# A GNN kernel's fused stage: each gather on GpSimd waits until the one two places ahead has landed

## The reference

```python
# layer 0, edges with 64 features
messages = concat([x[senders], edges64]) @ W_message
agg = segment_sum(messages, receivers)
h = layer_norm(relu(agg) + x) ; nodes = mlp_with_skips(h, 3 layers)
x1 = layernorm(x + layer_norm(x + nodes))
# layer 1, edges with 128 features: attention over the neighbours
h = lrelu(x1 @ w_W + w_b) ; edge_h = lrelu(edges128 @ ew_W + ew_b)
e_ij = concat([h[tgt], h[nbr], edge_h]) @ a_W + a_b
alpha = segment_softmax(e_ij, tgt)
out = layernorm(x1 + lrelu(segment_sum(alpha * h[nbr], tgt)))
```

## Time and profile before

| | |
|---|---|
| median of 3 runs | 6498.25 us (6482.75 to 6502.19) |
| span of the profiled execution | 6510.1 us |
| TensorE busy | 4187.0 us, 64% |
| VectorE busy | 3490.4 us, 54% |
| GpSimd busy | 3530.3 us, 54% |
| ScalarE busy | 1870.4 us, 29% |
| granted TensorE clock, mean | 0.820 of full speed |
| gathers of the fused stage (line 750) | 1785, 1789.7 us on GpSimd |

### The profile page before, as it was taken

How to read it: one execution, slowest core, us unless ns; L and a number is a source line. 1 busy time by engine, 2 the same in 40 slices (tenths; PEclk the granted TensorE clock), 3 DMA queues, 4 the chain that set the end, 5 groups by cost and what they waited for, 6 DMA issues and landing times. The chain is left out here.

```text
span 6510.1 us, 83702 instructions
## 1 busy us (share of the span) xinstructions
PE 4187.0 (64%) x17113; PEld 3084.5 (47%) x17114; DVE 3490.4 (54%) x11262; ACT 1870.4 (29%) x5506; POOL 3530.3 (54%) x3618
## 2 busy tenths in 40 slices
PE   3767777776777777777777835555555555555555
PEld 2545555554555545555555524444444444444444
DVE  6555556555555555565556644444444444444444
ACT  2222222222222222222222213333333333333333
POOL 3555555554555545555555426666666666666664
PEclk8888888988898888888888867777777777777777
DMA  3444444443444434444444623333333333533332
GB/s 115 116 115 119 113 117 125 116 115 111 120 116 119 118 110 116 113 122 114 114 116 125 110 62 91 92 91 91 92 90 92 93 92 90 91 90 93 91 91 69
DMA packets 546631, 679.29 MB, mean 104 GB/s; under 512 B 341873, under 2 KB 379359, under 8 KB 546221
## 3 DMA queue, kind: packets, MB, share of 16 engines
q0 software_dynamic: 172416, 464.26, 26.7%
q1 hardware_dynamic: 359216, 201.09, 11.8%
q10 hardware_dynamic: 14976, 13.69, 0.6%
HBM read 648.41 MB, written 29.43 MB: 104 GB/s over the span
## 5 line engine op out<-in xcount | busy, mean ns | idle before, releaser
L750 POOL DMA_INDIRECT rows<-in_x,picked x1785 | 1789.7, 1003 | 1692.3 <-ACT picked L942 1138.5
L1658 POOL DMA_INDIRECT nbr<-nodetab,nbr_idx x1700 | 1609.8, 947 | 1030.1 <-issue 460.5
L781 PE MATMUL bank<-w_edge,feats 128*128 128x258 f32 x3264 | 1122.3, 434 | 631.0 <-ACT bank L923 360.4
L796 PE MATMUL bank<-rows,hot 128*128 128x320 f32 x3570 | 1358.4, 480 | 54.2 <-issue 47.3
L1688 PE MATMUL bank<-nbr,w 128*128 128x258 f32 x3400 | 1044.3, 471 | 289.2 <-issue 152.6
L923 ACT COPY bank<-b_edge 128x258 f32<-128x258 f32 x1635 | 610.4, 378 | 2113.9 <-DVE unused L1151 1597.1
L1151 DVE SCALAR_TENSOR_TENSOR unused<-bank,a_relu 128x258 bf16<-128x258 f32 x1632 | 686.2, 422 | 952.3 <-remote 522.8
L1688 PEld LDWEIGHTS bank<-nbr,w 128*128 128x128 f32 x3400 | 803.3, 244 | 487.6 <-issue 195.5
L781 PEld LDWEIGHTS bank<-w_edge,feats 128*128 128x128 f32 x3264 | 622.9, 213 | 861.1 <-ACT bank L923 416.5
L1720 ACT ACTIVATE w<-off,logit 128x128 f32<-128x128 bf16 x1700 | 523.6, 388 | 1490.5 <-DVE logit L1791 1146.8
L796 PEld LDWEIGHTS bank<-rows,hot 128*128 128x128 f32 x3570 | 759.4, 214 | 277.0 <-issue 126.4
(11 more groups left out here) (347 smaller groups left out, 3943.4 us busy)
## 6 DMA issues: line engine op xcount, KB each, us to landing
feats<-in_edge SPq DMA_DIRECT2D x408, 256.0 KB
rows<-in_edge SPq DMA_DIRECT2D x255, 128.0 KB, 2.6
rows<-in_x,picked POOLq DMA_INDIRECT x1785
nbr<-nodetab,nbr_idx POOLq DMA_INDIRECT x1700
rows<-in_edge SPq DMA_DIRECT2D x153, 160.0 KB
nodetab<-tab ACTq DMA_DIRECT2D x52, 129.0 KB
x_blk<-in_x SPq DMA_DIRECT2D x52, 128.0 KB
x_rows<-u_n ACTq DMA_DIRECT2D x52, 128.0 KB
```

Source lines behind the costliest of these rows:

```text
L750: pool.indirect_dma_start(out=rows[:, STARTS[j] + s, 0:D], out_offset=None, in_=a["x"], in_offset=bass.IndirectOffsetOnAxis(ap=picked[j][: ...
L781: mm(y, feats[:, f0 * P:(f0 + 1) * P], w_edge[:], start=False, stop=True, skip_group_check=True).then_inc(o["y_ready"], 1)
L796: ins = mm(S_PS, hot[j % HR][:, s - STARTS[j], :], rows[:, s, :], start=(s == 0), stop=(s == SA - 1), skip_group_check=True)
L1658: pool.indirect_dma_start(out=nbr[:, TOFF[u] + k, :], out_offset=None, in_=nodetab, in_offset=bass.IndirectOffsetOnAxis(ap=nbr_idx[u][:, k ...
```

## The change

The semaphores of the gathers no longer belong to batches. There are five, used in turn: gather `s` of a pass (0 to 34) adds to `x_in[s % 5]`. 35 is a multiple of five, so each semaphore rises by 112 a pass, and `landed(p, s)` gives the semaphore and the count at which gather `s` of pass `p` has landed. Before each gather but the first two of a pass GpSimd waits for `landed(p, s - 2)`. TensorE waits before a batch for its last two gathers, in place of the batch's one count.

```diff
-            x_in = [sem(f"x_in{j}", ctx) for j in range(NB_SUMS)]
+            x_in = [sem(f"x_in{r}", ctx) for r in range(5)]
...
+            UNDER_WAY, XR = 2, 5
+            assert SA % XR == 0 and UNDER_WAY < XR
...
+            def landed(p, s):
+
+                return x_in[s % XR], p * (SA // XR * 16) + (s // XR + 1) * 16
...
                 def gathers(p, *batches):
                     for j in batches:
                         wait_alone(pool, (o["picked_ready"], p * NB_SUMS + (j + 1)), (o["summed"], p * NB_SUMS + (j + 1)))
-                        for s in range(SUMS[j]):
+                        for s in range(STARTS[j], STARTS[j] + SUMS[j]):
+                            if s >= UNDER_WAY:
+                                wait_alone(pool, landed(p, s - UNDER_WAY))
                             pool.indirect_dma_start(
-                                out=rows[:, STARTS[j] + s, 0:D], out_offset=None, in_=a["x"],
-                                in_offset=bass.IndirectOffsetOnAxis(ap=picked[j][:, s:s + 1].bitcast(U32), axis=0),
-                            ).then_inc(x_in[j], 16)
+                                out=rows[:, s, 0:D], out_offset=None, in_=a["x"],
+                                in_offset=bass.IndirectOffsetOnAxis(ap=picked[j][:, s - STARTS[j]:s - STARTS[j] + 1].bitcast(U32), axis=0),
+                            ).then_inc(x_in[s % XR], 16)
...
                         if s == STARTS[j]:
-                            size = SUMS[j] * 16
-                            pe.wait_ge(x_in[j], p * size + size)
+                            for last in range(s + SUMS[j] - UNDER_WAY, s + SUMS[j]):
+                                pe.wait_ge(*landed(p, last))
                             pe.wait_ge(e_in[j], p * 16 + 16)
```

## The result

The changed kernel takes 6438.12 us (median of 4 runs, 6430.82 to 6451.28) against 6500.22 us (4 runs, 6482.75 to 6507.75): ratio 0.9911, 95% interval 0.9891 to 0.993. The change saves 62 us, 0.9%, where 530 were forecast, over eight times as much. The time lies inside the range given, 5740 to 6800, but only because that range was stretched to a rival's price; the range of the forecast's own mechanism, 5740 to 6210, is missed. Its profiled execution has a span of 6439.0 us, 71.1 less than before.

What follows compares the result with a forecast made beforehand. Slow spells beside GpSimd's gather runs were taken to set the 71.5 us pass. 49 x (71.5 - 61.0) = 515 us, first pass 25, stage's end -10: together 530 off 6510.1, 5980 profiled, say 5970; range 5740 to 6800.

Steps and rivals of the forecast that it cites:

- (a): GpSimd's gathers waiting for the landing two places ahead: 1.56 to 1.81 us each against 1.25, 56.6 to 65.4 a pass.
- the pair: Two gathers on GpSimd take one landing, 2.35 to 2.85 us, plus one start, 0.77: 3.12 to 3.62 us.
- (b): If a fused-stage pass stayed at 71.5 us, the gathers' waits would be hidden in slack and the time unchanged.
- (c): Wait instructions: free on GpSimd; TensorE's eight more a pass cost 0 to 40 us, taken as 0.
- (d): Slow spells of TensorE beside GpSimd's gather runs cost 18.0 us a pass and all but vanish when runs are broken.
- The drain of 1.65 us a gather: Each gather leaves something that drains at a fixed rate, 1.65 us a gather; a cadence about that slow avoids spells.
- First and last pass: Fused stage's ends: 25 us gained in the first pass, 10 us lost where the DMA engines are full at the end.
- The slower one: Rival: spells ignore short pauses and last as long as GpSimd works; 77.2 us a pass, 6780 us; chance 0.33.
- Its other form: No spell, but landing plus start over 4.0 us pushes a pass past 71.5 us; within the slower side's 0.33.
- No change: Rival: spells hang on the gathers' number or the code's place, not spacing; 6480 to 6518 us, chance 0.13.
- Half the gain: Rival: spells get shorter but stay, 65.5 to 71 us a pass; 6210 to 6478, about 6340 us; chance 0.12.
- The rule of the Trainium skill: A DMA never contends with a compute engine, so gathers cannot hold up TensorE and the time would stay; ranked below.

Runs made afterwards that it cites:

- e3_one: The changed kernel with each gather waiting for the one just ahead, on a chip without spells: 8874.14 us, 1.7959 of the kernel before.
- e6_two: The changed kernel itself, two gathers under way, on a chip without spells: 5895.78 us against 4941.78 for the kernel before, ratio 1.1931.
- Four under way: The changed kernel with gathers waiting for the one four ahead, on a chip without spells: 4912.66 us, 0.9941 of the kernel before.
- e15: The kernel before without its fused stage's gathers, on a chip with spells: 5423.05 us against 6512.17, ratio 0.8334.
- Breaks: The changed kernel, only each batch's first gather waiting two ahead, others four: 5231.7 us (1.0587 of before) without spells, 6156.98 (0.9463) with.
- e12: The changed kernel, only each batch's first gather waiting two ahead, others four, on a chip without spells: 5231.7 us, 1.0587 of the kernel before.
- thirds: The changed kernel, every third gather waiting two ahead, others four, on a chip with spells: 5960.34 us, 0.9344 of the kernel before.
- narrow: The changed kernel gathering 64 of 256 columns, on a chip with spells: 6099.85 us, 0.9549 of the kernel before.
- three under way: The changed kernel with gathers waiting for the one three ahead: 5103.6 us (1.0327 of the kernel before) without spells, 6231.77 (0.9796) with.
- e5_before: The kernel before, unchanged, traced on a chip without spells: 4937.47 us in one run.

## Why the prediction was right or wrong

**(a) GpSimd's cost of a gather under the waits: wrong, and the step that failed.** Forecast 1.56 to 1.81 us a gather and a pass of 56.6 to 65.4, measured 1.93 and 70.2. The term is the pair: 3.12 to 3.62 us forecast, 3.86 measured (2 x 1.93). A lone one takes 3.5 to 3.58 (e3_one), inside the forecast. I had added a landing and a start from two single rows of the kernel before and taken the sum to hold for two under way; with two it does not hold, and steps of 3.56 stand beside steps of 4.18. What lengthens them is not shown. The scatters were not sized too small. Among passes 6 to 49 two gathers take 3.94 us where no scatter stands between them and 4.48 where one does, so a scatter adds some 0.5 us and not the 1.0 forecast, and the pass is 35 x 1.97 + 2 x 0.5 = 70. The 9 us a pass above the forecast 61 are the gathers' alone. In the span, 459 us are missing (5980 forecast, 6439 measured), and 49 passes of 69.9 instead of 61 are 438 of them. The upper ends, 65.4 and 6210 us, would still have been 228 us off. (By the terms written out, 56.6 and 65.4 us a pass give 5753 and 6184, not 5740 and 6210; nothing hangs on it.)

**(b) Hidden if a pass stayed at 71.5.** Not tested as such: the pass is GpSimd's. That rests on e6_two, where nothing else can hold it: 69.5 us with a free pass of 50.

**(c) The waits as instructions cost nothing: right.** Four under way has nearly all the waits and takes what the kernel without gathers takes, 4912.66 and 4913.08 us.

**(d) The slow spells: cause and price right, the condition roughly, on this kind of chip.** The gathers cause them (e15). Their price was put at 18.0 us a pass from one last pass; it is 71.1 - 50.2 = 20.9. They go when the stream thins: no "remote" waits in the changed kernel, excess 0.7 us. The drain of 1.65 us a gather was worked out from two runs of rows; that the runs bear it out roughly is more than two rows could promise. Breaks at (1828.2 + 925.8) / 1785 = 1.54 us a gather (e12) still has an excess, thirds at (1814.5 + 1205.0) / 1785 = 1.69 has three tenths of the "remote" waits left, narrow at 1.77 has 11 us of them from 400 to 2600 us, the changed kernel none. Whether anything drains no run shows. What was not seen is that they do not exist on the other kind of chip, where the same change is pure loss.

**First and last pass.** The first came 26.0 us earlier, forecast 25. The end cost 28.2 us where 10 were put: TensorE waits in the last pass for gathers that were issued as late as in any other, and loses its short pass of 53.5 us. The stage's last gather started at 3714.69 us before, 4.8 us after the 50th closing line; now it starts 68.5 us after it, 13.2 us before the end of the last pass:

```profile
3675.60 0.95 POOL L758 DMA_INDIRECT rows<-in_x,picked  x1 [0.53 <-issue]
```

The two together are +2 us, forecast -15.

**The rivals.** The slower one (spells as long as GpSimd works) fell: the spells went. Its other form, no spell but landing plus start over 4.0 us, was missed narrowly, 3.86 us and two scatters making 70.2 of 71.5 us; this is where most of the gain went. "No change" fell by mechanism. "Half the gain" covers the time, 6210 to 6478, but its mechanism, shorter spells, is not what happened here; it is what three under way and breaks do. The rule of the Trainium skill weighed there ("SBUF — State Buffer", "Who interferes with whom"), that a DMA does not contend with a compute engine, fits the chips where the gathers cost 31 us of 4944. Where they cost 1089 of 6512 something that this rule leaves out holds the engines up; that it is a port of the SBUF no run shows.

## What to carry to other kernels

A throttle's cost is the cycle of what it waits for, divided by the number under way, but the cycle changes with that number: it was 3.58 us with one, 3.86 with two, 4.4 with three. Measure it at the number you mean to use; landing and start taken from single rows gave 9 us a pass too little here. When the aim is to thin a stream, waiting at every third item costs less than waiting at every one (61.7 us a pass against 70.2) and took most of the spells away. Spread the waits evenly: with about the same mean pace, but all of the waits for the second one ahead in one half of the pass, 65.6 us were left. And take the profile on more than one chip before tuning against a stall whose cause is not in the program: here the same edit is worth -0.9% and +19.3%.

## What the runs showed of the hardware

Chips of two kinds run one program in 4942 and in 6364 to 6512 us, 29 to 32% longer, and the difference hangs on GpSimd's gathers beside the engines' work: without them the fused stage agrees to 0.2 us. What a spell is, is open. The prediction described it by TensorE's weight loads, but in the kernel before it does not begin there. Timelines of TensorE and VectorE in the slow step of the earlier trace rows:

```profile
1660.03 1.05 PE L855 MATMUL bank<-h_t,w_mlp 128*128 128x128 f32 x8
1660.91 0.60 PE L781 MATMUL bank<-w_edge,feats 128*128 128x258 f32 x2
```

```profile
1660.01 0.68 DVE L1171 TENSOR_TENSOR hot<-iota,rel 128x512 f32<-128x512 f32 x1
1666.10 0.61 DVE L1218 SCALAR_TENSOR_TENSOR h_t<-bank,b_low,s_t 128x128 f32<-128x128 f32 x2 [5.40 <-remote]
1666.62 0.41 DVE L1151 SCALAR_TENSOR_TENSOR unused<-bank,a_relu 128x258 bf16<-128x258 f32 x1
```

VectorE stands still for 5.4 us, though what lines 1218 and 1151 read is ready at about 1661.1 and 1661.5 (the ends of matmuls are modelled). TensorE's loads 0.71 us apart come after that. Nor is it TensorE's clock: in that stretch TensorE is busy 6.00 of 6.00 us at a granted clock of 1.00. The window's row (us, busy of PE, PEld, DVE, ACT, POOL, PEclk, DMA share, GB/s):

```profile
1660.00:1666.00 6.00, 6.00 (x36) 4.43 (x34) 0.69 (x2) 0.02 (x1) 4.78 (x5) 1.00 0.48 134
```

Over 400 to 2600 us the granted clock is 0.86 in the kernel before, 0.98 on a chip without spells (e5_before) and in e15, and 0.88 to 0.89 in the changed kernel on both kinds. So it is low in the changed kernel too, where there are no spells, and what share of the 20.3 us excess is the lower clock's was not measured.

An engine that cannot go on though its input is there could lack its next instructions. The Trainium skill's "Runtime: NRT & Kernel Launch", "Instruction fetch mechanics", says that each engine refills a small instruction memory in blocks over a DMA queue of its own, and that this is mostly hidden. This trace speaks against it. The profile of the kernel before has two queues of the kind "instruction", in the page and in the end of the stage, 3700 to 3800 us:

```profile
q8 instruction: 7, 0.11, 0.0%
q14 instruction: 16, 0.13, 0.0%
...
q8 instruction: 1, 0.02, 0.1%
q14 instruction: 2, 0.02, 0.1%
```

From 160 to 3700 us, through some 50 passes with all their spells, neither moves a packet; the only queues are

```profile
q0 software_dynamic: 88063, 232.66, 23.8%
q1 hardware_dynamic: 291556, 166.67, 18.1%
q10 hardware_dynamic: 14112, 12.90, 1.1%
```

Only a fetch that the profile does not record could still be late. Two things about the gathers were left untested as well: e15 takes away the making of the descriptors and the moving of the data together, and no run has narrow gathers at full pace. The earlier trace rows speaks against the data, with the DMA engines 0.94 busy, GpSimd idle and TensorE at full work.
